# Attention in a gated layer: exponentials as the stationary operand of the values' product

## The reference

```python
# x, ctx: (32, 128, 128); 16 heads of 8
h = layernorm(x)
q, k, v = heads(h @ Wq + bq), heads(ctx @ Wk + bk), heads(ctx @ Wv + bv)
a = softmax(q k^T * 8**-0.5)
x = x + tanh(g_xattn) * ((a v) @ W_out + b_out)
# then a mixture of experts: 8 experts, top 1, capacity 512 of the 4096 tokens
t = layernorm(x); gates = softmax(t @ Wg); e = argmax(gates)
slot = running count of earlier tokens of the same expert; dropped from 512 on
x = x + tanh(g_ffn) * gate * (relu(t @ W1[e] + b1[e]) @ W2[e] + b2[e])
```

## Time and profile before

| | us |
|---|---|
| profiled execution, own time | 371.71 |
| its span, first to last instruction | 369.9 |
| median of three runs | 377.73 |
| TensorE busy | 269.8 (73%) |
| VectorE busy | 230.8 (62%) |
| POOL busy | 173.4 (47%) |
| ScalarE busy | 155.9 (42%) |
| mean granted TensorE clock | 0.873 |

### The profile page before, as it was taken

The page is one execution under the profiler, slowest core; times in us unless marked ns, Lnnn a source line. Parts: engine busy times, 40 slices in busy tenths (PEclk is TensorE's granted clock), DMA queues, the critical chain, the costliest instruction groups (busy, mean ns, idle before and its releaser), DMA issues.

```text
span 369.9 us, 8316 instructions
## 1 busy us (share of the span) xinstructions
PE 269.8 (73%) x3024; PEld 175.0 (47%) x3024; DVE 230.8 (62%) x712; ACT 155.9 (42%) x325; POOL 173.4 (47%) x200
## 2 busy tenths in 40 slices
PE   0638477698797698788699798986830599999930
PEld 0224244355464465555465465643520257677730
DVE  6666857979987959799698697941411034544430
ACT  7223146356475456467276565762100132232100
POOL 3364822715637707727646917052075004455662
PEclk9998579989999969899789999996555599999985
DMA  3983845224126123332431432028011524656310
GB/s 87 307 194 110 238 125 164 83 75 132 48 56 189 36 70 95 110 87 81 124 83 50 133 89 88 5 81 181 0 51 61 143 58 135 176 160 197 83 40 20
DMA packets 48535, 39.26 MB, mean 106 GB/s; under 512 B 9618, under 2 KB 44071, under 8 KB 48496
## 3 DMA queue, kind: packets, MB, share of 16 engines
q1 hardware_dynamic: 44784, 28.67, 28.8%
q0 software_dynamic: 3712, 10.07, 8.6%
HBM read 13.72 MB, written 12.65 MB: 71 GB/s over the span
## 4 chain that ended last, share of the span: by engine, by line
issue 24%; PE 22%; POOL 21%; DVE 12%; DMA 10%; SPq 4%; ACT 4%; POOLq 1%; DVEq 0%; ACTq 0%
DMA rec_dram<-rec,slot 6%; POOL rec_dram L990 6%; POOL out_dram L1044 6%; DVE xn L777 4%; PE O L473 3%; DVE negm L702 3%; DMA qp<-mrow 2%; SPq L307 2%; PE X L501 2%; PE S L443 2%; PE X L401 2%; PE TS L458 2%; POOL parts_k L251 2%; POOL rest_k L248 2%; PE X L418 2%
## 5 line engine op out<-in xcount | busy, mean ns | idle before, releaser
L702 DVE TENSOR_REDUCE negm<-S 128x4 f32<-128x512 f32 x128 | 81.7, 680 | 15.3 <-PE S L443 14.0
L599 ACT ACTIVATE prob<-TS 128x512 f32<-128x512 f32 x128 | 69.6, 598 | 34.5 <-PE TS L458 34.5
L473 PE MATMUL O<-prob,vals 128*32 128x128 f32 x1024 | 58.9, 304 | 0.0
L458 PE MATMUL TS<-qp,kp 64*128 64x128 bf16 x512 | 30.1, 232 | 16.1 <-DMA qp<-mrow 15.5
L990 POOL DMA_INDIRECT rec_dram<-rec,slot x32 | 31.8, 995 | 11.2 <-issue 11.2
L1044 POOL DMA_INDIRECT out_dram<-fin,tok x32 | 31.4, 981 | 11.2 <-issue 11.2
L443 PE MATMUL S<-kp,qp 62*128 62x128 bf16 x512 | 32.4, 231 | 2.5 <-DVE negm L702 2.3
L248 POOL TENSOR_TENSOR rest_k<-full_k,parts_k 128x512 f32<-128x512 f32 x7 | 8.1, 1155 | 55.2 <-ACT parts_k L591 55.2
L458 PEld LDWEIGHTS TS<-qp,kp 64*128 64x128 bf16 x512 | 20.0, 101 | 20.9 <-DMA qp<-mrow 18.8
L556 PE MATMUL X<-w2s,qp 128*128 128x128 f32 x256 | 29.7, 275 | 0.0
L963 POOL TENSOR_TENSOR fence_p<-pool_c 128x1 f32<-128x1 f32 x16 | 3.1, 194 | 56.5 <-DVE fin L943 34.1
(11 more groups left out here) (112 smaller groups left out, 527.5 us busy)
## 6 DMA issues: line engine op xcount, KB each, us to landing
kp<-parts_k SPq DMA_DIRECT2D x48, 128.0 KB
qp<-parts_q SPq DMA_DIRECT2D x48, 128.0 KB, 2.4
rec_dram<-zeros POOLq DMA_DIRECT2D x8, 516.0 KB
xr<-rec_dram SPq DMA_DIRECT2D x8, 260.0 KB, 2.9
c_sb<-in_ctx_dram SPq DMA_DIRECT2D x8, 256.0 KB, 4.4
out_dram<-rec SPq DMA_DIRECT2D x8, 256.0 KB, 2.5
w1s<-in_L_ffn_W_dram SPq DMA_DIRECT2D x8, 256.0 KB, 3.1
w2s<-in_L_ffn_W_dram SPq DMA_DIRECT2D x8, 256.0 KB, 2.7
```

Source lines behind the costliest of these rows:

```text
L458: mm = nc.tensor.matmul(TS[:, a, i * L:(i + 1) * L], kp[b][rows, h, t0:t0 + L], qp[b][rows, h, t0:t0 + L], start=True, stop=True)
L473: mm = nc.tensor.matmul(O[i * HV:(i + 1) * HV, n % 2, q * L:(q + 1) * L], vals[G % 2][:, k, h, :], prob[n % 2][:, h * L:(h + 1) * L], star ...
L599: nc.scalar.activation(prob[n % 2][:, first:first + 4 * L], TS[:, a, :], ACT.Exp).then_inc(a_exp, 1)
L702: V.tensor_reduce(negm[n % 2][:, first:first + 4], S[:, a, :].rearrange("p (h k) -> p h k", k=L), AX.X, ALU.max, negate=True).then_inc(v_r ...
```

## The change

The values product is turned round. `prob` of a head (128 x 128) is the stationary operand, and the head's eight value columns and the column of ones move; the result has the queries on the partitions and lies in O at 16 columns per head. So the raw copy by ScalarE and the back-transposition by TensorE are gone, and `normalise` reads O. O has one bank in place of two. The bank that comes free, M, takes the maxima's transposition and the small transposition, and no longer X. On TensorE the maxima's transposition stands right behind the first half of the shifted scores, on VectorE `normalise` stands first in its step. The padding of the value columns with zeros is gone. The experts' hidden products use O and M.

```diff
-    HV = 32
+    HV = 16
@@ banks
-        O = ps("O")
+        O = ps("O", 1)
+        M = ps("M", 1)
-        oraw = [sb(f"oraw{i}", [P, 4 * L]) for i in range(2)]
@@ order of the banks' uses
-            bank0 = [("at", c - 5), ("m", c - 1), second]
-            bank1 = [first, ("back", c - 4), third, ("oT", c - 4)]
+            bank0 = [("at", c - 5), second]
+            bank1 = [first, third]
+            bank2 = [("m", c - 1), ("oT", c - 4)]
+        m_out = M[:, 0, 0:P // 2].bitcast(BF16)[0:2 * HEADS, :]
+        oT_out = M[:, 0, P:P + L]
+        o_out = O[:, 0, 0:2 * P]
@@ TensorE, values
-                q = 2 * a + u
-                    if n >= 2:
-                        pe.wait_ge(a_O, n - 1)
+                    if n >= 1:
+                        pe.wait_ge(v_on, n)
                 for i in range(4):
-                    h = 4 * q + i
-                    mm = nc.tensor.matmul(O[i * HV:(i + 1) * HV, n % 2, q * L:(q + 1) * L], vals[G % 2][:, k, h, :],
-                                          prob[n % 2][:, h * L:(h + 1) * L], start=True, stop=True)
+                    h = 8 * a + 4 * u + i
+                    mm = nc.tensor.matmul(o_out[:, h * HV:h * HV + HD + 1], prob[n % 2][:, h * L:(h + 1) * L],
+                                          vals[G % 2][:, k, h, 0:HD + 1], start=True, stop=True)
@@ TensorE, step: behind shifted(c - 2, 0)
+                if is_batch(c - 1):
+                    bank_free(pe, "m", c - 1)
+                    pe.wait_ge(v_m, c)
+                    nc.tensor.transpose(m_out, mpart[(c - 1) % 2][:].rearrange("p a j h -> p (a j h)"),
+                                        ident_b[:]).then_inc(p_m, 1)
@@ TensorE, step: gone from behind values(c - 3, 0, 0)
-                if is_batch(c - 4):
-                    bank_free(pe, "back", c - 4)
-                    pe.wait_ge(a_O, c - 3)
-                    for i in range(4):
-                        mm = nc.tensor.transpose(X[:, 1, i * L:(i + 1) * L], oraw[c % 2][:, i * L:(i + 1) * L], ident)
-                    mm.then_inc(p_back, 1)
@@ ScalarE, step: gone from its start
-                    nc.scalar.activation(oraw[n % 2][:], O[:, n % 2, :], ACT.Copy).then_inc(a_O, 1)
@@ VectorE
             def normalise(n):
-                o = X[:, 1, :].rearrange("p (h v) -> p h v", v=HV)
-                dve.wait_ge(p_back, n + 1)
+                o = o_out.rearrange("p (h v) -> p h v", v=HV)
+                dve.wait_ge(p_O, n + 1)
             def step(c):
+                if is_batch(c - 4):
+                    normalise(c - 4)
                 if is_batch(c):
                     top(c, 0)
...
-                if is_batch(c - 4):
-                    normalise(c - 4)
@@ experts' hidden products
-                    bank = (TS if f % 2 == 0 else O)[:, f // 2, :]
+                    bank = (TS[:, 0, :], O[:, 0, :], TS[:, 1, :], M[:, 0, :])[f]
```

More of the change, by code:

```diff
@@ L60, in sb, with ps @@
             return ctx.enter_context(nc.sbuf_tensor(name, shape, dt))
-        def ps(name):
-            return ctx.enter_context(nc.psum_tensor(name, [P, 2, 512], F32))
+        def ps(name, banks=2):
+            return ctx.enter_context(nc.psum_tensor(name, [P, banks, 512], F32))
         def sem(name):
@@ L173, in flamingo_kernel @@
         p_cT, p_xT, p_q, p_k, p_v = sem("p_cT"), sem("p_xT"), sem("p_q"), sem("p_k"), sem("p_v")
-        g_zero = sem("g_zero")
         g_vals, a_pad, v_pad = sem("g_vals"), sem("a_pad"), sem("v_pad")
-        p_back, a_O = sem("p_back"), sem("a_O")
         p_S, p_m, p_T, p_O, p_oT, p_at = sem("p_S"), sem("p_m"), sem("p_T"), sem("p_O"), sem("p_oT"), sem("p_at")
@@ L207, in is_group @@
             return 0 <= g < NG
-        BATCH_TASKS = ("m", "at", "back", "oT")
+        BATCH_TASKS = ("m", "at", "oT")
         def x_tasks(c):
@@ L218, in x_tasks @@
             second = {1: ("nT", g - 2), 2: ("xT", g + 2), 3: ("q", g + 2)}.get(j)
-            bank0 = [("at", c - 5), ("m", c - 1), second]
-            bank1 = [first, ("back", c - 4), third, ("oT", c - 4)]
+            bank0 = [("at", c - 5), second]
+            bank1 = [first, third]
+            bank2 = [("m", c - 1), ("oT", c - 4)]
             ok = lambda t: t is not None and (is_batch(t[1]) if t[0] in BATCH_TASKS else is_group(t[1]))
-            return [[t for t in bank0 if ok(t)], [t for t in bank1 if ok(t)]]
+            return [[t for t in bank if ok(t)] for bank in (bank0, bank1, bank2)]
         before = {}
-        for bank in range(2):
+        for bank in range(3):
             last = None
@@ L232, in flamingo_kernel @@
         emptied = {"v": v_v, "cT": a_cT, "k": a_kf, "lg": v_lg, "pos": v_pos, "nT": a_nT, "xT": a_xT, "q": a_qf,
-                   "m": a_m, "at": v_x1, "back": v_on, "oT": a_oT}
+                   "m": a_m, "at": v_x1, "oT": a_oT}
+        m_out = M[:, 0, 0:P // 2].bitcast(BF16)[0:2 * HEADS, :]
+        oT_out = M[:, 0, P:P + L]
+        o_out = O[:, 0, 0:2 * P]
         def bank_free(eng, name, idx):
@@ L478, in step @@
             def step(c):
-                todo = x_tasks(c)[::-1 if c < 0 else 1]
+                todo = x_tasks(c)[:2][::-1 if c < 0 else 1]
                 groups = [t for bank in todo for t in bank if t[0] not in BATCH_TASKS]
@@ L522, in step @@
                     pe.wait_ge(v_on, c - 3)
-                    nc.tensor.transpose(X[:, 1, 0:L], on[c % 2][:], ident).then_inc(p_oT, 1)
+                    nc.tensor.transpose(oT_out, on[c % 2][:], ident).then_inc(p_oT, 1)
                 if is_batch(c - 3):
@@ L623, in step @@
                         act.wait_ge(m_in[n % 2], 32 * (n // 2))
-                    nc.scalar.activation(mrow[n % 2][:], X[:, 0, 0:P // 2].bitcast(BF16)[0:2 * HEADS, :],
-                                         ACT.Copy).then_inc(a_m, 1)
+                    nc.scalar.activation(mrow[n % 2][:], m_out, ACT.Copy).then_inc(a_m, 1)
                 if j == (3 if g + 2 else 2) and is_group(g + 2):
@@ L646, in step @@
                         act.wait_ge(p_at, n - 1)
-                    nc.scalar.activation(onT[n % 2][:], X[:, 1, 0:L], ACT.Copy).then_inc(a_oT, 1)
+                    nc.scalar.activation(onT[n % 2][:], oT_out, ACT.Copy).then_inc(a_oT, 1)
                 if j == 3 and is_group(g + 2):
@@ L923, in relus @@
                         load_b1(e + 1)
-                    V.tensor_scalar(hid[p][:, f, :], O[:, f // 2, :], b1_dve[p][:, 0, f:f + 1], 0.0, ALU.add, ALU.max).then_inc(v_H, 1)
+                    V.tensor_scalar(hid[p][:, f, :], (O if f == 1 else M)[:, 0, :], b1_dve[p][:, 0, f:f + 1], 0.0, ALU.add, ALU.max).then_inc(v_H, 1)
             def load_b1(e):
@@ L1028, in _ @@
             for i in range(2):
-                G_.memset(vals[i][:, :, :, HD:HV], 0.0).then_inc(g_zero, 1)
-            pool.wait_ge(g_zero, 2)
-            for i in range(2):
                 G_.memset(vals[i][:, :, :, HD:HD + 1], 1.0).then_inc(g_vals, 1)
```

## The result

The changed kernel takes 513.59 us at the median (508.33 to 514.9, four runs) against 377.88 us: a ratio of 1.3744, 95% interval 1.3656 to 1.3833. It is slower by 136 us. The forecast was 472 us in a range of 415 to 525; the time lies inside the range, on the side of the rival "half clock throughout" (527 us).

The account below looks back on a forecast made before the run. TensorE's in-order stream was taken to set the pace. Five groups +51.5, the next +18.4, the stretch to the last values product +20.8, the start +4: 371.7 to 466.4, plus 6.0 for the median: 472 us, range 415 to 525.

Parts of the forecast that it names:

- half clock throughout: Rival: TensorE stays at half clock through the attention stage; +149 us, 527 us in all; chance 0.12.
- The stream: TensorE's work per attention group of four batches: from 20.9 us to 28.5 at full clock, replacing a 28.5 us period.
- bounds for a record: Values product, per record: 24 to 30 ns below, 206 ns above; 122 ns taken from the fp32 router product.
- The clock: Attention stage: long loads lose TensorE's full clock; half clock 0.6 of the time, 0.9 without k and q.
- since only the steps with k, q and v have wide products: Reason given for taking 0.6 of the time at half clock in the attention groups, 37.8 us per group.
- The mixed clock: Main case: attention alternates between half and full clock; 472 us, running from about 435 to 510; chance 0.60.
- the held clock: Rival: the clock stays full in the attention stage; +16 us, 394 us in all; chance 0.12.
- Zero for the maxima's transposition: Attention steps: its 16.4 us of idle go, as values blocks cover the scatters; 2 to 5 us a group otherwise.
- The 1 us per group for the normalisation: Attention steps: TensorE waits for VectorE to normalise the single-buffered O; 1 us per group, between 0 and 4.
- +4 forecast for the way to the second group's v: The two batches before 62.9 us: eight dearer values blocks less what goes, +4 us.
- The waits stay: Rival: waits behind the scatters or at the single O remain; 4 us more for six groups, 496 us; chance 0.11.
- the loads hide: Rival: values loads run ahead beside the former product, a block falls to 0.19 us; about 350 us; chance 0.05.

Follow-up runs that it names:

- e7_fill4: Changed kernel plus four extra bf16 products of 256 moving columns ahead of each values block, same output: 455.4 us, ratio 1.217 to the kernel before.
- e1_wide: Changed kernel with each values product moving 128 columns instead of nine, same loads, wrong output: 405.5 us, ratio 1.042 to the kernel before.
- e3_bf16: Changed kernel with exponentials and values in bf16 instead of fp32: 374.8 us, ratio 0.962 to the kernel before.
- e4_mmove: Kernel before, old values product kept, with only one bank of O, bank M and the early maxima's transposition: 388.3 us against 391.6.
- e2_fill: Changed kernel plus two extra bf16 products of 256 moving columns ahead of each values block: 511.8 us, 1.31 against the kernel before.
- e10_bfsp: Changed kernel with bf16 exponentials and values, and SP issuing the maxima's DMA ahead of the part packing: ratio 1.006 to the kernel before.
- e11_oldsp: Kernel before, still fp32, with only SP's order changed, the maxima's DMA ahead of the part packing: 394.0 us against 377.8.

## Why the prediction was right, and where it was off

**The stream.** The forecast summed a group's stream to 28.5 us at full clock and 48.3 at half, 43.3 without k and q, and 60.3 to the last values product. At a clock of 0.50 to 0.51 the kernel measures 46.9, 43.6 and 60.5. Of the bounds for a record, the one taken was right in kind: the row of the same type and shape. Its size at full clock was 122 ns forecast and 111 measured (e7_fill4); at half clock 206 forecast and 206 to 215 measured. The Trainium skill, "TensorE: Matmul & The Clock Gate", section "LDWEIGHTS (loading the stationary operand)", takes a load's columns over 1.2 GHz: 107 ns for 128 columns, an estimate from the page. The trace agrees at full clock (111 ns a record), and differs at half clock, where the record takes 206 to 215 ns.

**The clock: the term that was mis-sized.** The forecast took 0.6 of the time at half clock in the groups with k and q and 0.9 behind them; measured are 0.98 (clock 0.51) and all of it. That is +92.0 where 51.5 was forecast for the five groups, and +21.5 and +24.8 where 18.4 and 20.8 were. The step that failed is "since only the steps with k, q and v have wide products": I took these steps to get their clock back, and they hardly did. The direction of the argument was right and is now shown, by e1_wide and e7_fill4: the same loads with more moved columns run at 0.89 and 0.83 in the mean. The mixed clock was said to give 435 to 510 us, so the measured 513.6 us is not a case of it; that the range still took it in is owed to the margin up to 525, and is luck more than reasoning.

In size, the held clock was forecast at +16 us, a ratio of 1.042, and e1_wide, which holds it nearly, measures 1.042 (1.034 to 1.051). By that some 16 of the 136 us are the loads net of the waits that went, and some 120 are the clock. This is an estimate: the two ratios come from two chips, e1_wide pays for its wider moves as well, and against the fastest run of the kernel before on its chip it is 1.066. That the two ratios agree to the last digit is chance.

**Waits.** Zero for the maxima's transposition was right in number (0.3 us), but the reason that was given, the earlier place and the values blocks as cover, is only part of it. Where TensorE has time to spare, the new order leaves about half or more: 10.4 us before the maxima's transposition in e3_bf16 and 7.9 in e4_mmove, of 16.4; 15.0 and 9.1 for the DMA of the maxima, of 15.5. e3_bf16 differs from the changed kernel in the operands' type alone, so in the changed kernel these waits are hidden behind a TensorE that comes late, not removed. The 1 us per group for the normalisation was too much: with the stream at half clock VectorE is in time. Under a full clock it is real (6.8 us over e1_wide, 1.43 in its row). Nothing but 7.0 us of DMA, 2.7 before the scores and some single waits at the start and end are left as idle of TensorE in the changed kernel.

**Start and expert stage.** +4 forecast for the way to the second group's v, +7.7 measured, with the granted clock at 0.55 from 35 us on. 0 forecast behind the last values product, -3.2 measured. The last 69.9 us, with the experts, are alike (TensorE busy 54.5 us in both kernels), so the 3.2 us lie ahead of them; their cause was not looked for.

**Rivals.** "The waits stay" and "the loads hide" are refuted by the rows; "half clock throughout", at 0.12, is what came: 527 forecast, 513.6 measured. Of the 13 us between them some 7 come from the step to the median of the runs: 6.0 us were added for it, and the median of the changed kernel lies 1.3 us under its profiled execution. The other 6 are in the sum: 99 us for the five groups, where 92.0 were measured, and the two ends (+4 and 0, measured +7.7 and -3.2), which cancel. It deserved more weight: the earlier trace rows held a stretch of 8.80 us with k-less steps in which the clock never came back, with loads busy in 5.32 us of it; in the changed kernel they are busy in 213.19 of 234.56 us.

What stays open: why two extra products a block (e2_fill) leave the clock alternating and four hold it in most of the stage was measured, not explained; and what bounds the turned bf16 kernel, since its clock was raised without gain and its DMA wait only exchanged for another.

## What to carry to other kernels

When operands are swapped, price the load as well as the moved columns. Here the fp32 load of 128 columns set the price of a record, so that nine moved columns took 0.89 us a block and 128 took 0.98, and the four strips side by side (0.36 us) were lost. A stream of long loads and short moves can be busy all the time and still lose the clock; look in the trace before for a busy stretch at half clock and ask what moved in it. And before an order is changed to remove a wait, name what then comes late: in three kernels (e4_mmove, e10_bfsp, e11_oldsp) a wait was shortened and came back elsewhere. A wait that has gone from the profile need not have been removed either: the engine that used to wait may just have become slower.

## What was not expected of the hardware

TensorE was busy for 338.5 of 338.6 us, 234.56 of 234.56 us in the first stretch, at a granted clock of 0.51. The Trainium skill, "TensorE: Matmul & The Clock Gate", section "Part 1: The HAM clock gate (the "warmup" mystery)", ties the clock to how busy the engine has recently been. In the sense of the profile's busy time this trace disagrees. In e1_wide, with the same number of values records and loads, the clock is at 0.97 in its window: what decided there was how many columns moved. Adding 512 products of 256 columns to a kernel bound by TensorE took it from 513.6 to 455.4 us.
